# Reordering one step of VectorE and one step of GpSimd in a one-core attention and FFN kernel

## What is computed

```python
x = x + attention(layernorm(x))     # rms norm with gamma, qkv product, softmax(q k^T / 8) v, output product
x = x + ffn(layernorm(x))           # gelu(x w1 + b1) w2 + b2, scaled by the sum of the two renormalised router weights
```

## Time and profile before

| | |
|---|---|
| median of 3 runs | 1263.11 us (1261.81 to 1264.73) |
| the profiled execution | 1262.66 us, of which the traced span is 1260.8 us |
| mean granted TensorE clock | 0.991 |
| PE busy | 1192.6 us (95%) |
| DVE busy | 969.6 us (77%) |
| ACT busy | 900.8 us (71%) |
| POOL busy | 635.6 us (50%) |
| chain that ended last | PE 69%, DVE 14%, ACT 7%, POOL 5%, issue 4%, DMA 1% |

### The profile page before, as it was taken

How to read it: one execution, slowest core, us unless ns; L and a number is a source line. 1 busy time by engine, 2 the same in 40 slices (tenths; PEclk the granted TensorE clock), 3 DMA queues, 4 the chain that set the end, 5 groups by cost and what they waited for, 6 DMA issues and landing times.

```text
span 1260.8 us, 29220 instructions
## 1 busy us (share of the span) xinstructions
PE 1192.6 (95%) x11328; PEld 1053.7 (84%) x11328; DVE 969.6 (77%) x1738; ACT 900.8 (71%) x1925; POOL 635.6 (50%) x796
## 2 busy tenths in 40 slices
PE   4788999999999999999999999999999988999998
PEld 3677888888888888888888888888888877898887
DVE  4678888878887888888887888788878875666654
ACT  3677888788878887888788878887888784344432
POOL 2345555555555556555555555555555575222221
PEclk8899999999999999999999999999999999999999
DMA  4112211221122112211221121112111222202100
GB/s 152 26 43 51 52 35 34 69 51 35 35 68 51 35 35 68 51 35 41 64 50 37 42 64 46 41 41 64 43 41 43 66 61 67 68 34 67 34 18 34
DMA packets 31656, 62.91 MB, mean 50 GB/s; under 512 B 5664, under 2 KB 7968, under 8 KB 31520
## 3 DMA queue, kind: packets, MB, share of 16 engines
q1 hardware_dynamic: 31520, 61.05, 19.0%
HBM read 19.08 MB, written 8.39 MB: 22 GB/s over the span
## 4 chain that ended last, share of the span: by engine, by line
PE 69%; DVE 14%; ACT 7%; POOL 5%; issue 4%; DMA 1%; DVEq 0%; POOLq 0%; ACTq 0%
PE ps L425 35%; PE ps L483 14%; PE ps L469 9%; PE ps L441 7%; ACT prob L702 5%; DVE negmax L947 5%; DVE pT_lo L879 5%; PE ps L445 3%; POOL prob L782 3%; DVE nat L879 1%; ACT nat L671 1%; POOL wbig_lo L826 1%; POOL att_hi_v L802 1%; POOL attT_lo L808 1%; DVE ln_var L860 1%
## 5 line engine op out<-in xcount | busy, mean ns | idle before, releaser
L782 POOL TENSOR_SCALAR prob<-prob,rowinv 128x512 f32<-128x512 f32 x512 | 348.8, 695 | 375.6 <-DVE rowinv L952 375.1
L702 ACT ACTIVATE prob<-ps,negmax 128x512 f32<-128x512 f32 x512 | 346.9, 684 | 58.5 <-DVE negmax L947 53.9
L879 DVE TENSOR_TENSOR pT_lo<-ps,pT_hi 128x512 fp32r<-128x512 f32 (+1 forms) x384 | 320.5, 862 | 26.5 <-ACT pT_hi L695 11.9
L947 DVE TENSOR_REDUCE negmax<-ps 128x2 f32<-128x1024 f32 x256 | 309.6, 1209 | 0.2 <-PE ps L445 0.2
L469 PEld LDWEIGHTS ps<-identity,prob 64*128 64x128 f32 x4096 | 160.0, 140 | 99.0 <-POOL prob L782 62.0
L469 PE MATMUL ps<-identity,prob 64*128 64x64 f32 x4096 | 179.9, 227 | 43.0 <-DVE vbuf L879 19.4
L692 ACT ACTIVATE pT_hi<-ps 128x1024 fp32r<-128x1024 f32 x128 | 131.4, 1027 | 106.6 <-issue 102.4
L441 PE MATMUL ps<-nat 64*128 64x512 f32 x1024 | 177.3, 417 | 0.4 <-ACT prob L702 0.4
L483 PE MATMUL ps<-pT_hi,vbuf 128*128 128x256 f32 x1024 | 164.2, 282 | 1.2 <-DVE pT_lo L879 1.2
L483 PE MATMUL ps<-pT_lo,vbuf 128*128 128x256 f32 x1024 | 164.2, 283 | 0.0
L483 PEld LDWEIGHTS ps<-pT_hi,vbuf 128*128 128x128 f32 x1024 | 144.3, 189 | 7.5 <-DVE pT_lo L879 2.0
(11 more groups left out here) (108 smaller groups left out, 2269.9 us busy)
## 6 DMA issues: line engine op xcount, KB each, us to landing
att_hi_v<-halves_out SPq DMA_DIRECT2D x128, 128.0 KB, 2.3
att_lo_v<-halves_out SPq DMA_DIRECT2D x128, 128.0 KB, 2.4
xin<-in_x SPq DMA_DIRECT2D x8, 512.0 KB, 3.8
xres<-in_x SPq DMA_DIRECT2D x8, 512.0 KB, 3.6
x_scratch<-xres SPq DMA_DIRECT2D x8, 512.0 KB, 3.1
out_y<-f_o SPq DMA_DIRECT2D x16, 256.0 KB, 2.0
prob<-in_w_qkv SPq DMA_DIRECT2D x5, 512.0 KB, 4.5
wstage<-in_w SPq DMA_DIRECT2D x4, 512.0 KB, 3.9
```

The source lines that it names most:

```text
L702: act.activation(prob[:, n % NPROB, j * SEQ:(j + 1) * SEQ], ps[:, PS_SCORE[n % 2] + j, :], ACT.Exp, bias=negmax[:, n % 4, j:j + 1], accum_ ...
L782: return pool.tensor_scalar(dst, src, scalar, 1.0, ALU.mult, ALU.mult)
L879: return dve.tensor_tensor(dst, full, hi, ALU.subtract)
L947: dve.tensor_reduce(negmax[:, n % 4, :], ps[:, PS_SCORE[n % 2]:PS_SCORE[n % 2] + 2, :], AX.X, ALU.max, negate=True).then_inc(s_max, 1)
```

## The change

On DVE, `slot_tasks(2s)` moves from before `row_inverse(2s)` to near the end of the step, after the first auxiliary blocks, and `row_max(2s+1)` now comes before `row_inverse(2s)` instead of after it. On POOL, in even steps, `attention_out` now comes before `normalise_prob(2s-1)` instead of after it. No operation is added or removed, and no other engine's list changes.

```diff
@@ GpSimd
             for step in range(FIRST_STEP, LAST_STEP + 1):
+                if step % 2 == 0 and 0 <= step // 2 - 2 < NPAIR:
+                    attention_out(step // 2 - 2)
                 if 0 <= 2 * step - 1 < NUNIT:
                     normalise_prob(2 * step - 1)
-                if step % 2 == 0 and 0 <= step // 2 - 2 < NPAIR:
-                    attention_out(step // 2 - 2)
                 if 0 <= 2 * step < NUNIT:
                     normalise_prob(2 * step)
@@ VectorE
                 if 0 <= 2 * step - 2 < NUNIT:
                     transposed_lo(2 * step - 2)
-                slot_tasks(2 * step)
+                if 0 <= 2 * step + 1 < NUNIT:
+                    row_max(2 * step + 1)
                 if 0 <= 2 * step < NUNIT:
                     row_inverse(2 * step)
-                if 0 <= 2 * step + 1 < NUNIT:
-                    row_max(2 * step + 1)
                 for block_of_aux in aux_of(step)[0]:
                     aux_done(*block_of_aux)
+                slot_tasks(2 * step)
                 slot_tasks(2 * step + 1)
```

## The result

| | before | changed |
|---|---|---|
| median of the runs | 1263.78 us (1261.81 to 1264.73) | 1304.80 us (1302.48 to 1314.78) |
| the profiled execution | 1262.66 us, span 1260.8 | 1304.18 us, span 1302.4 |
| mean granted clock | 0.991 | 0.982 |

The change makes the kernel 3.4% slower: the ratio is 1.034, with a 95% interval of 1.030 to 1.039. The forecast was 1298 us, with a range of 1285 to 1310 us.

The account below looks back on a forecast made before the run. The prediction took PE to bound a steady batch. POOL's +44.2 us less DVE's 3.5, 1.3, 1.6 and 4.2 gave +33.6, with 1 for slow DMAs +35 on 1262.66; it forecast 1298 us, range 1285 to 1310.

Parts of the forecast that it names:

- 36 ordinary and short pairs: Pairs of heads without special work: 29 ordinary +17.4 us, 7 lasting 15.01 us +5.7, and 13 for slow DMAs.
- 8 input pairs: Pairs with the next batch's transposed input, 17.57 us: POOL's loop costs 0, two waits on exp(2s+1) shrink, -1.6 us.
- The loop, T + 11.04 + 4.78 = 15.82 us: From an odd step's start T, attention_out starts 11.04 us later, the next T 4.78 behind that; 15.21 us before.
- Late DMAs land on PE's path: Before attention_out on POOL: of the idle time at slow DMAs, 13 us now delays PE in 36 pairs.
- VectorE's gain in ordinary pairs: Even steps: PE idles 0.12 us less as row_max moves, 6.4 us alone, taken as 0 behind POOL's loop.
- First layernorm pair to 15.82 us: Moved statistics end PE's 1.12 us wait; 16.41 us falls to 15.82, -4.7 over eight, -3.5 after a slow DMA.
- Ramp 2.1 us for each of two: Ramp slots 6 and 10, w_out low parts delaying PE 3.63 us: 2.1 us less for each, -4.2 us.
- The later reciprocal is covered: DVE's reciprocal of unit 2s comes about 1 us later; PE has 2.4 us of cover, 1.4 left, no cost.
- The last pair: T 3.2 us later, and 1.4 us behind it: Last odd step starts at 1048.92 instead of 1045.76, +3.2 us; weight split behind one more normalisation, +1.4.
- The clock holds: PE's granted clock stays up behind the new waits; 0.73 with the 15.8 us loop; below 0.98 in steady batches means wrong.
- the rival with the falling clock: PE's granted clock falls behind long new waits: 1.6 us each, +8 for five, 1306 us; if all, 1370; chance 0.08.
- GpSimd's part alone: POOL's reordering without DVE's gains: 40.7 us, and 8 x 0.44 for second layernorm pairs, makes 44.2 us.

Follow-up runs that it names:

- e4: The changed kernel with the addition of line 802 left out of attention_out, DMAs and their wait kept: 1247.94 us, 0.986 of before.
- e7: The changed kernel with one more copy of 0.62 us in attention_out on POOL: 1358.72 us, 1.078 of before.
- e8: The changed kernel with two more copies of 0.62 us in attention_out on POOL: 1421.29 us, 1.124 of before.
- e1: The kernel before with only VectorE's (DVE's) new order, GpSimd's (POOL's) loop as before: 1240.70 us, 0.982 of before.
- e2: The kernel before with only attention_out moved ahead of normalise_prob(2s-1) on GpSimd (POOL), VectorE's order as before: 1319.97 us, 1.044 of before.

## Why the prediction was right, and where it was off

The time was forecast 7 us too low, within the range. In the traces the changed kernel reached its last T 41.4 us later than the kernel before (its span grew by 41.6). By kind, in us:

| | forecast | measured |
|---|---|---|
| 36 ordinary and short pairs | +36.1 | +40.6 |
| 8 first layernorm pairs | -3.5 | -1.6 |
| 8 second layernorm pairs | +2.2 | +5.0 |
| 8 input pairs | -1.6 | -0.7 |
| ramp | -4.2 | -3.4, and -1.7 ahead of the first T |
| the last pair, and what follows its T | +4.6 | +3.2 |
| late DMAs of layernorm pairs | +1.0 | in their rows |

- *The loop, T + 11.04 + 4.78 = 15.82 us.* Right, to 0.02 us: undisturbed pairs take 15.80 us, `attention_out` starts at T + 11.03 (166.31 to 177.34) and the next T follows 4.77 us later. e4, e7 and e8 show that it is a loop and that its terms add. That the way from T to the DMA's landing would not shorten when PE waits was right as well.
- *Late DMAs land on PE's path.* Right. In the 36 ordinary and short pairs of before, 12.5 us of lateness stood in this path (measured by the starts that lie more than 0.3 us beyond T + 11.04). In the changed kernel it is 12, once the 6 us are taken off by which the clock had made four of these pairs' even steps late. The forecast had 13. What makes these DMAs late was not tried.
- *VectorE's gain in ordinary pairs is 0.12 us and is worth nothing behind the loop.* The second half was right. The first was too small: e1's ordinary pairs go from 15.22 to 15.03 us, 0.19 us. The idle piece of the earlier trace rows was not all that the wait cost.
- *First layernorm pair to 15.82 us.* Right: 213.75 to 229.55 is 15.80 us. Two of the eight (17.3 us each) met late DMAs, which is why their sum is smaller.
- *Ramp 2.1 us for each of two.* The right waits, put a little too high: the wait at the start of step 4 is 1.84 us instead of 3.63, and the two pairs are shorter by 1.6 and 1.8 us. The first T lay 1.7 us sooner as well, but over the ten kernels it lies anywhere from 48.0 to 50.4 us, in no order that an edit explains.
- *The later reciprocal is covered.* Right in ordinary and layernorm pairs: neither in e1 nor in the changed kernel does PE wait before the second transposition of an even step there. In the input pairs that wait, which was 0.68 us, has grown to 0.86 in most of e1's and to 1.03 in the changed kernel, while the one ahead of the first transposition has shrunk by more (0.67 to 0.20 in e1). But the reciprocal is later by only 0.5 us, not by 1: POOL's normalisation of unit 2s ends at T + 7.79 (174.10), where it ended at T + 7.31. The forecast did not take off the 0.38 us that the reciprocal had waited anyway, nor that the work before it now starts 0.2 us sooner. So POOL's idle time before line 802 is 3.24 us and not 2.7.
- *The last pair: T 3.2 us later, and 1.4 us behind it.* The size is partly luck. The last T came 3.1 us later, but PE did not wait for GpSimd there: the normalisation was done at 1086.74, which would have let T come at about 1086.8, and PE started at 1087.17 without a bracket. PE's own work ended last, slowed by a clock that fell behind a wait of 2.33 us for ACT's copy (line 712). What follows T took 0.1 us more, so no run shows the 1.4.
- *The clock holds.* This is the step that was off. The forecast had no term for the clock; it gave the rival with the falling clock (1306 us) a chance of 0.08, and that is the one that the measurement, 1304.80, is nearest to. In six pairs the clock fell behind a wait of 2.0 to 2.3 us and the even step began about 1.5 us late, 9 us together; the rival had +8 for five. Without these 9 us the growth would be 32 us, against the sum of +34.6: the other terms were together 2 us too high. So with a term for the clock the forecast would have been about 2 us too high; without one it was 7 us too low. Over whole batches the mean granted clock is 0.99 or 1.00 in six of seven; the last, with two falls, has 0.97, under the 0.98 that the prediction named as a sign of being wrong.
- *GpSimd's part alone +44.2 us, VectorE's alone about -25.* The experiments measured +56 and -23. In the trace of e2 eight even steps began late behind a fall of the clock, 12 us together, which is about the difference.

The clock's rows stand best at one place in the changed kernel: a late DMA made PE wait for 2.25 us, and the transpositions behind it took 1.11 us.

```profile
278.56 0.71 PE L469 MATMUL ps<-identity,prob 64*128 64x64 f32 x16
...
295.89 1.11 PE L469 MATMUL ps<-identity,prob 64*128 64x64 f32 x16 [2.25 <-POOL prob L782]
...
304.96 0.71 PE L469 MATMUL ps<-identity,prob 64*128 64x64 f32 x16
...
313.28 0.71 PE L469 MATMUL ps<-identity,prob 64*128 64x64 f32 x16 [0.78 <-POOL prob L782]
```

Busy time by stretch from there (the last three numbers are clock, DMA share, GB/s):

```profile
295.80:297.00 1.20, 1.11 (x18) 1.11 (x20) 0.00 (x0) 0.00 (x0) 1.20 (x3) 0.54 0.00 0
297.00:299.00 2.00, 2.00 (x12) 1.55 (x12) 1.29 (x3) 1.09 (x2) 1.51 (x3) 0.50 0.00 0
299.00:301.00 2.00, 2.00 (x28) 1.75 (x25) 1.13 (x1) 0.82 (x1) 0.00 (x0) 0.92 0.00 0
301.00:303.00 2.00, 2.00 (x19) 2.00 (x19) 1.69 (x2) 2.00 (x7) 0.00 (x0) 1.00 0.03 8
```

The granted clock is at its lower level, 1.2 GHz, for some 3.4 us of this, and the even step begins 9.07 us behind T instead of 7.54. The 1.5 us pass through the loop like any other: `attention_out` starts at T + 12.60, and this pair takes 17.39 us although its DMAs were on time. A late DMA can so be paid for twice, once by the wait and once by the clock of the next pair.

The trace of before could not show this: its waits at the start of a step were 0.4 to 1.9 us, at a held clock, or 3.63 us, with a fall. The new waits lie between, and I priced the gap with the nearer end.

## What to carry to other kernels

Before an operation is moved ahead of another on an in-order engine, ask what it waits for, and who waits for what then stands behind it. A wait that another engine's slack had hidden turns into a loop as soon as the thing behind it feeds what the wait comes from, and its length against the bound engine's time per turn decides: e4's 14.4 us cost nothing where the DMAs were punctual, 15.8 us cost 0.6 to 0.8 us a turn.

Blocks that are not urgent (layernorm, weights) belong behind those that the next step waits for; and a chain with a DMA at its head belongs where the DMA is long done, even if its engine has idle time sooner. Two edits with opposite signs can hide in one change: here -23 and +56 us.

## What the runs showed of the hardware

The granted clock fell behind waits of PE that were shorter than I had thought. I counted PE's waits at the start of odd steps (the length of a pair less PE's own time) and whether the even step then began late by more than 0.7 us. In the changed kernel, of 9 waits of 1.8 to 2.8 us 6 were followed by a fall, of more than 40 waits of 0.3 to 1.8 us none. In e8, of some 40 waits of 1.8 to 2.8 us (nearly all 2.2 us) 11 were followed by one, and of 12 longer ones 10. So at about 2.2 us the length of the wait alone does not decide.

The ramp shows the same for waits at the start of even steps, which this count leaves out: behind 1.84 us at step 4 the clock fell in the changed kernel and held in e4. Busy time by stretch, the changed kernel first, then e4 (the third number from the end is the clock):

```profile
56.70:58.70 2.00, 1.94 (x22) 1.88 (x24) 1.48 (x3) 1.91 (x6) 0.00 (x0) 0.57 0.55 117
```

```profile
56.50:58.50 2.00, 1.95 (x28) 1.86 (x30) 1.68 (x3) 1.97 (x6) 0.00 (x0) 1.00 0.56 119
```

The pair took 17.07 us with the fall and 15.54 without it. So 1.84 us is not safe either, although in before 1.89 us had passed at a held clock.

This fits the wider spread of the kernels with waits of about 2 us: before spans 3 us and e1 3 us in four runs, the changed kernel 12, e2 14, e7 18, e8 10. The mean granted clock of the runs goes with it (changed kernel: 0.986 in the fastest run, 0.979 in the slowest). That the clock makes the whole of the spread is not shown, since only one execution of each kernel has a trace.

The Trainium skill (TensorE: Matmul & The Clock Gate, HAM oscillation) says that idle gaps between bursts throttle TensorE, and that the next burst begins slow. The rows agree: 1.11 us for transpositions that take 0.71, behind 2.25 us of waiting; behind another wait of 2.25 us (362.35) they took 0.71.
